# Regrouping the first chunk pair's preparation in an RWKV and Hadamard-MLP kernel: the second chunk's token statistics and normalisation move around the first weight pass, and other steps move with them

## The reference

```python
xn = _layernorm(x)
# attention: token shift, three projections, a running recurrence along the tokens
xr = mu_r * xn + (1 - mu_r) * shifted;  xk = ...;  xv = ...
r, k, v = xr @ Wr.T, xk @ Wk.T, xv @ Wv.T            # 512 x 512 each
wkv = wkv_v4(k, v, wkv_w, wkv_u)                     # max-stabilised scan over the tokens
att = (sigmoid(r) * wkv) @ Wo.T
# MLP: two up projections to 2048, silu gate, Walsh-Hadamard transform, down projection
hidden = fwht(silu(xn @ W1.T) * (xn @ W3.T))
ffn = hidden @ W2.T
out = x + att + ffn
```

## Time and profile before

| | |
|---|---|
| time, median of 3 runs | 2727.08 us (2725.96 to 2729.17) |
| the profiled execution's own time | 2726.61 us |
| its span in the profile | 2724.8 us |
| PE busy | 2665.6 us, 98% |
| DVE busy | 2205.9 us, 81% |
| ACT busy | 1318.0 us, 48% |
| POOL busy | 243.0 us, 9% |
| first product of the first pair starts | 129.99 us into the span |

### The profile page before, as it was taken

One profiled execution on the slowest core, in us unless ns is written; L12 is line 12 of the kernel. 1 busy time (PEld: TensorE's weight loads), 2 busy tenths in 40 slices (PEclk: granted clock), 3 DMA queues, 4 the chain that ended last, 5 costly groups with the idle time before them and its releaser, 6 DMA issues.

```text
span 2724.8 us, 33882 instructions
## 1 busy us (share of the span) xinstructions
PE 2665.6 (98%) x11616; PEld 2181.7 (80%) x11616; DVE 2205.9 (81%) x2962; ACT 1318.0 (48%) x2115; POOL 243.0 (9%) x180
## 2 busy tenths in 40 slices
PE   7998999999999999999999999999999999999999
PEld 5676778888888888888888888888888888888887
DVE  6798987888878888688886888878888788878775
ACT  6655556444544445444464444644455444554442
POOL 3297820000000000000000000000000000000000
PEclk9999999999999999999999999999999999999999
DMA  6787687787878778687787877878687787876777
GB/s 237 279 309 246 239 284 251 251 263 232 273 240 274 241 244 283 226 276 241 250 280 230 269 235 263 271 238 272 220 276 251 250 264 228 272 244 222 226 233 266
DMA packets 244951, 691.50 MB, mean 254 GB/s; under 512 B 31920, under 2 KB 31920, under 8 KB 244272
## 3 DMA queue, kind: packets, MB, share of 16 engines
q1 hardware_dynamic: 244784, 689.34, 76.2%
HBM read 575.94 MB, written 113.30 MB: 253 GB/s over the span
## 4 chain that ended last, share of the span: by engine, by line
PE 87%; DVE 8%; ACT 2%; issue 2%; DMA 1%; POOL 1%; SPq 0%; ACTq 0%; DVEq 0%
PE gamma L863 12%; PE gamma L865 12%; PE gamma L866 12%; PE acc L873 10%; PE acc L875 10%; PE acc L874 10%; PE gamma L945 4%; PE gamma L947 4%; PE gamma L946 4%; PE alpha L866 2%; PE alpha L865 2%; PE alpha L863 2%; PE alpha L946 1%; PE alpha L947 1%; PE alpha L945 1%
## 5 line engine op out<-in xcount | busy, mean ns | idle before, releaser
L1059 ACT ACTIVATE step<-gamma 128x512 f32<-128x512 f32 x512 | 305.7, 597 | 840.9 <-PE gamma L866 817.9
L863 PE MATMUL gamma<-xs_high,wring 128*128 128x512 f32 x1280 | 500.2, 391 | 14.2 <-DVE step L1514 8.3
L865 PE MATMUL gamma<-xs_high,wring 128*128 128x512 f32 x1280 | 498.9, 390 | 0.0
L866 PE MATMUL gamma<-xs_low,wring 128*128 128x512 f32 x1280 | 498.8, 390 | 0.0
L873 PE MATMUL acc<-vring,hid 128*128 128x512 f32 x1232 | 481.5, 391 | 14.2 <-POOL vring L744 6.7
L875 PE MATMUL acc<-vring,hid 128*128 128x512 f32 x1232 | 479.9, 390 | 0.0
L874 PE MATMUL acc<-vring,hid 128*128 128x512 f32 x1232 | 479.9, 390 | 0.0
L863 PEld LDWEIGHTS gamma<-xs_high,wring 128*128 128x128 f32 x1280 | 240.9, 188 | 69.3 <-issue 11.2
L873 PEld LDWEIGHTS acc<-vring,hid 128*128 128x128 f32 x1232 | 231.3, 188 | 68.9 <-issue 14.8
L866 PEld LDWEIGHTS gamma<-xs_low,wring 128*128 128x128 f32 x1280 | 240.8, 188 | 50.2
L865 PEld LDWEIGHTS gamma<-xs_high,wring 128*128 128x128 f32 x1280 | 240.9, 188 | 49.8
(11 more groups left out here) (171 smaller groups left out, 4779.8 us busy)
## 6 DMA issues: line engine op xcount, KB each, us to landing
wring<-u_split SPq DMA_DIRECT2D x336, 512.0 KB, 4.2
vring<-d_split SPq DMA_DIRECT2D x288, 512.0 KB, 4.3
wring<-r_split SPq DMA_DIRECT2D x168, 512.0 KB, 4.2
raw<-spilled SPq DMA_DIRECT2D x160, 256.0 KB, 4.2
spilled<-step SPq DMA_DIRECT2D x128, 256.0 KB, 4.3
wlast<-u_split SPq DMA_DIRECT2D x112, 256.0 KB, 3.3
u_split<-wring SPq DMA_DIRECT2D x48, 512.0 KB, 3.3
res<-x SPq DMA_DIRECT2D x16, 1024.0 KB, 8.0
```

The costliest lines, as they stand in the source:

```text
L863: pe.matmul(bank[:, :], w[:, 0, col], high, start=fresh and kt == 0, stop=False, skip_group_check=True)
L865: pe.matmul(bank[:, :], w[:, 1, col], high, start=False, stop=False, skip_group_check=True)
L866: last = pe.matmul(bank[:, :], w[:, 0, col], low, start=False, stop=kt == 1, skip_group_check=True)
L1059: act.activation(to, bank[:, :], ACT.Copy).then_inc(u_copied, 1)
```

## The change

No operation is added or taken away: all five engines issue the same work, and SP's list is the same row for row. What moves, all of it in the prologue:

1. The second chunk's statistics (`first_stats(1)`) are issued on DVE after step 1, not ahead of step 0. Its diagonals on ACT come after steps 3 and 4, behind the emptying of the first group, not after step 1. Its spreading matmuls come after pass one, not after unit 4, and wait for pass one's banks to be copied. Its `centre` and `scale` move behind stages 3 and 4 of the recurrence, and `mix_first(0, 12)` with them. Pass one waits for two normalised column pairs (`xt_ready`), no longer four.
2. POOL makes the low parts of weight tiles 4 to 8 ahead of its second reciprocal root, not behind it. ACT's high parts go out in another order (tile 2 behind the first high part of the mix, one tile a step, tiles 9 to 11 at steps 6 to 8).
3. Stages 5 and 6 of the recurrence's first quarter move behind steps 10 and 11. The rectification stands after tile 2 of pass one (3 before) and tile 1 of pass two (3 before), the exponentials after tiles 6 and 5 (9 before).
4. `right_made` is issued one piece a step behind steps 17 to 20 (two pieces at 16, one at 17 and at 18 before), `right_lo` at steps 21 to 23. `right_hi` keeps its places. Each product of up step 0 waits only for the right operand that it reads.

```diff
-FIRST_MADE_AT = {16: (0, 1), 17: (2,), 18: (3,)}
+FIRST_MADE_AT = {17: (0,), 18: (1,), 19: (2,), 20: (3,)}
 FIRST_HIGH_AT = {15: (0,), 16: (1,), 17: (2, 3), 18: (4,), 19: (5,), 20: (6,)}
-FIRST_LOW_AT = {18: (0,), 19: (1,), 20: (2,), 21: (3,), 22: (4, 5), 23: (6,)}
+FIRST_LOW_AT = {21: (0, 1), 22: (2, 3), 23: (4, 5, 6)}
...
             inverse_root(0, 0)
             for n in range(12):
                 lo(("r", n))
-                if n == 3:
+                if n == 8:
                     inverse_root(0, 1)
...
+                if j == 0:
+                    wait(pe, xs_hi, s, RIGHT_ORDER.index(RIGHT[piece]) + 1)
+                    wait(pe, xs_lo, s, RIGHT_ORDER.index(RIGHT[piece]) + 1)
                 if piece == 1:
                     if j == 0:
-                        wait(pe, xs_hi, s, 7)
-                        wait(pe, xs_lo, s, 7)
...
             def spread_tokens(h):
                 for a in range(2):
+                    if h:
+                        pe.wait_ge(w2_copied, FT - 1 + a)
...
             def turn_within_tiles():
-                wait(pe, xt_ready, 0, 4)
+                wait(pe, xt_ready, 0, 2)
...
                 r_unit(0, n)
-                if n == SPREAD_AFTER:
-                    spread_tokens(1)
                 if n == PASS_ONE_AFTER:
                     turn_within_tiles()
+                    spread_tokens(1)
...
             mix_first(0, 1)
+            mix_second(0, 0)
             split_high(("r", 2))
-            mix_second(0, 0)
...
                 down_step(-1, n)
                 if n < 3:
-                    split_high(("r", 6 + 2 * n))
-                    split_high(("r", 7 + 2 * n))
-                if n == 1:
-                    diagonals_b(0)
-                    diagonals_b(1)
+                    split_high(("r", 6 + n))
+                if n in (3, 4):
+                    diagonals_b(n - 3)
+                if 6 <= n < 9:
+                    split_high(("r", 3 + n))
...
-                        if j == 3:
+                        if j == 2:
                             rectified(0, 0)
-                        if j == 9:
+                        if j == 6:
                             exponentials(0, 0)
+                    mix_first(0, 12)
...
-                if not with_d and n in (PASS_ONE_AFTER + 1, PASS_TWO_AFTER + 1):
+                if not with_d and n == PASS_ONE_AFTER + 1:
+                    wkv(r, 0, 3)
+                    wkv(r, 0, 4)
+                    centre(r, 1, 0)
+                    scale(r, 1, 0)
+                    mix_item(r, 12)
+                    centre(r, 1, 1)
+                    scale(r, 1, 1)
+                if not with_d and n == PASS_TWO_AFTER + 1:
                     for stage in range(3, 7):
-                        wkv(r, int(n > PASS_TWO_AFTER), stage)
+                        wkv(r, 1, stage)
...
+                    if not with_d and n == PASS_ONE_AFTER + 2:
+                        wkv(r, 0, 5)
+                    if not with_d and n == PASS_ONE_AFTER + 3:
+                        wkv(r, 0, 6)
...
             mix_item(0, 3)
-            first_stats(1)
             for n in range(R_UNITS):
                 down_step(-1, n)
+                if n == 1:
+                    first_stats(1)
```

More of the change, by code:

```diff
@@ L118 @@
 LOW_AT = {9: (0,), 11: (1,), 13: (2,), 16: (3,), 19: (4,), 20: (5,), 21: (6,)}
-SPREAD_AFTER, PASS_ONE_AFTER, PASS_TWO_AFTER = 4, 8, 14
+PASS_ONE_AFTER, PASS_TWO_AFTER = 8, 14
 TURN_ORDER = [W2_LOADS - 1] + list(range(W2_LOADS - 1))
@@ L953, in turn_across_tiles @@
             def turn_across_tiles():
+                wait(pe, xt_ready, 0, 4)
                 for n, j in enumerate(TILES_TURNED):
@@ L1231, in down_step @@
                         mix_second(r, n + MIX_AHEAD)
-                    if n + MIX_AHEAD + 1 < R_UNITS:
+                    if n + MIX_AHEAD + 1 < R_UNITS and (with_d or n != PASS_ONE_AFTER):
                         mix_first(r, n + MIX_AHEAD + 1)
@@ L1288, in _ @@
                         act.activation(fly[1][:, i, :], acc[i % TT][:, :], ACT.Copy).then_inc(w2_copied, 1)
-                        if k == 3:
+                        if k == 1:
                             rectified(0, 1)
-                        if k == 9:
+                        if k == 5:
                             exponentials(0, 1)
-                if n + 3 >= R_UNITS:
-                    split_high(("u", 0, n + 3 - R_UNITS))
+                if 0 <= n + 4 - R_UNITS < 3:
+                    split_high(("u", 0, n + 4 - R_UNITS))
             def pair(s):
@@ L1631, in down_step @@
                         add_residual(s, 0, ADD_A_AT[n])
-                if with_r:
-                    late = not with_d or is_first(s)
-                    centre_at, scale_at = (FIRST_CENTRE_AT, FIRST_SCALE_AT) if late else (CENTRE_AT, SCALE_AT)
+                if with_r and with_d:
+                    centre_at, scale_at = (FIRST_CENTRE_AT, FIRST_SCALE_AT) if is_first(s) else (CENTRE_AT, SCALE_AT)
                     if n in centre_at:
```

## The result

The changed kernel takes 2732.18 us, median of 20 runs (2729.72 to 2737.39), and the kernel before 2727.95 us in the same job (20 runs, 2724.28 to 2731.16). The ratio is 1.0016, 95% interval [1.001, 1.0023]: 4.2 us slower, where 1.9 us faster was forecast. It is within the 0.2% called "no difference" ahead of the run, but outside the range and on the other side. The profiled execution took 2731.28 us, its span is 2729.5 us, 4.7 us longer than before.

A forecast was written before the change was run, and what follows sets the result against it. PE was taken to pace the seven later pairs, DVE beside POOL the first; only the prologue could gain. Pass one 8.5 us ahead shrank to a first product 1.9 ahead: 2727.08 became 2725.2 us, range 2720.0 to 2728.6.

The forecast's parts named there:

- DVE's list between the passes: DVE's work from 61.4 us to the exponents of the second quarter at 84.8: 23.4 us, 2.5 ahead of before.
- The chain behind pass two: Serial ACT and DVE links behind unit 18: unit 20 starts at T + 18.8 after a 5.1 us wait, not 2.10.
- T: Start of unit 15, behind pass two: forecast at 96.7 us against 97.66 before, 1.0 ahead.
- Exponents of pass one: Ready on DVE at 49.5 us, between 47.5 free of POOL and 50.0 with both low parts held.
- The clock in the gap of pass one: PE's gap at tile 7, forecast at 2.3 us; no slow clock behind it in the sum.
- over 18 us: Sign on pass one's length: longer than this means the forecast is wrong on the slow side.
- The first product: First product of pair 0: forecast at T + 31.4 = 128.1 us, 1.9 ahead of 129.99.
- The later pieces find theirs with at most 0.5 of wait: In up step 0, products after the first wait at most 0.5 us for their right operands.
- DVE ends its seven low parts near T + 36: Right operands' low parts end 2 us later against the products, in a stretch where DVE was idle before.
- some 2 us: Allowance for contention of DVE and POOL in the first pair, which can add or take this much.
- Slower: PE's clock: Rival: two gaps inside the passes cost 1.7 us each, 1.5 slower, 2728.6 (0.10); lasting slow clock, 2741 (0.04).
- Nothing arrives: Rival: DVE paces the first pair from its first step, the 1.9 us is given back, 2727.1; chance 0.16.

The follow-up runs named there:

- e3: Changed kernel with the rectifications behind tiles 6 and 4 of the passes and the exponentials behind tiles 10 and 8: 2727.1 us against 2726.41 for the kernel before.
- e1: Changed kernel with sums and low parts of the right operands back at their old steps: 2721.89 us against 2726.41 for the kernel before.
- e2: Changed kernel with PE repeating tile matmuls in the gaps inside both passes: 2730.48 us against 2726.41 for the kernel before.
- e7: Changed kernel with the edits of e1 and e3 together: 2719.59 us against 2726.34 for the kernel before.
- e11: The e7 kernel with the last three `right_hi` one step later (steps 19 to 21): 2720.77 us against 2727.21 for the kernel before.
- e12: Changed kernel with `right_hi` one step later, each one step after the sum it needs (steps 18 to 21): 2731.28 us against 2727.21 for the kernel before.
- e13: Changed kernel with the edits of e9 and e12 together, sums still late: 2726.8 us against 2726.19 for the kernel before.
- e8: The e7 kernel with ACT's high parts of weight tiles 9 to 11 at steps 3 to 5, not 6 to 8: 2720.71 us against 2726.34 for the kernel before.
- e9: Changed kernel with only the low parts of the right operands back at their old steps, sums still late: 2730.52 us against 2726.34 for the kernel before.
- e10: Changed kernel with 20 unused matmuls on PE in the wait ahead of unit 20: 2732.98 us against 2727.21 for the kernel before.

## Why the prediction was wrong, point by point

**What held.** Unit 0 came at 16.52 (16.6 forecast), unit 4 without its wait, unit 5 at 33.06 behind 1.05 us (32.8, 1 us), pass one at 44.23 (44.0). DVE's list between the passes took 64.14 to 87.36, 23.2 us (23.4). The chain behind pass two came as worked out: unit 20 at T + 19.2 with a wait of 5.01 (T + 18.8, 5.1), T being unit 15's start. So the link-by-link walk of ACT and DVE was sound in these three stretches.

**What failed first: T, 3.3 us late (99.98 for 96.7).** The steps:
- Exponents of pass one at 50.73, not the 49.5 taken, and 0.7 outside the bounds of 47.5 to 50.0. The low parts of mixes 10 and 11 took 3.44 us for two, beside POOL, where the earlier trace rows have 0.68 for one alone. 1.2 us.
- The clock in the gap of pass one. The gap was 2.99 us (2.3 forecast), the clock share behind it 0.58. From the exponents to unit 9 it took 13.95 us, not 12.5; where the clock stayed up it took 12.67. 1.3 us.
- Unit 9's 2.7 us lateness moved the spreading of the second chunk and with it DVE's list one for one. Pass two lost another 0.7: from the exponents to unit 15 it took 12.62 us, not 11.9, and 11.33 where the clock stayed up. So the clock cost 1.3 us there too, and the forecast was 0.6 too long without it.

The clock's 2.6 us are most of T's 3.3. The forecast had its price in the earlier trace rows and put it in a rival only ("if each costs what the 2.10 us gap did"), with nothing in the sum. One of its own signs says the same: pass one took from 44.23 to 63.05, 18.8 us, where "over 18 us" was to mean wrong on the slow side. e3 prices the placement as a whole (7.2 us at unit 15).

**What failed second: behind unit 20.** The first product came at 132.97, 13.77 behind unit 20 and not 12.6: 1.2 us, for the slow clock lasted until about 125 us. With T's 3.3 and 0.4 in the chain that makes 4.9 us, from 1.9 ahead to 3.0 behind.

**What failed third, and weighs most in the runs:** "The later pieces find theirs with at most 0.5 of wait", and "DVE ends its seven low parts near T + 36 ... but it had an idle stretch there". The low parts ended at T + 40.6, since beside POOL's 512-column operations each takes 2.3 us and not 1.2 (13.0 for the seven, from 127.61). They cost 1.08 us in up step 0, and POOL's chain 2.69 at up step 1. The prediction allowed "some 2 us" for DVE and POOL in the first pair, outside its sum. Of the 6.65 us of lateness at up step 1, 4.7 are left at 172 us: the kernel before waited 1.36 us for a copy of ACT at 157.90, and the changed one, later already, didn't. The walk followed `right_made` to ACT's copies and stopped. It never asked what stands behind the *fourth* high part on ACT: the split of the first up weights, and behind that POOL's 17 us to up step 1. One engine's stand was costed for one reader and there were two. With both tables put back, e1 is 8.7 us faster, and its first product comes 5.3 us ahead of the kernel before.

**The rivals.** "Slower: PE's clock" named a real mechanism, at 1.7 us a gap where it cost 1.3, but with the clock held up (e2) no gain in the time can be told. "Nothing arrives" came closest: DVE and POOL are what the first pair waits for from its first step, as it said. Its price stopped at zero; being late against the products wasn't only the loss of a lead. The sign would have been right with the sums where they were: e1 is 4.5 us faster than before, though with 5.3 us of lead at the first product and not 1.9.

**What the loss consists of,** as far as the runs show: 8.7 us by the two tables (e1 against the changed kernel), some 3 by the placement of rectification and exponentials (3.5 by e3 against the changed kernel, 2.3 by e7 against e1, each uncertain by about as much), and a gain of 6.8 us by the rest, parts 1 to 3 with the per-product waits (e7). The rest was not taken apart: no run has part 1 or part 2 alone. The 8.7 don't look like a sum of parts: freeing ACT alone 0, spreading the low parts alone 0, both 3.6, and the sums early as well 8.7, each within 2.5 us or so.

**What stays open.** Why POOL took turns with DVE in the changed kernel, e1 and e7 and was shut out in e11, e12 and e13. The order of starting doesn't tell: POOL began 0.03 us ahead of a low part of DVE in e11 and 0.04 ahead of the same one in e7. Why e2 lost its 2.9 us between the first product and `vring`, and e12 5.4 us between up step 1 and `vring`. And why the same gap of PE, 2.99 us in the changed kernel and 2.96 in e1, was followed by a clock share of 0.58 in one and 1.00 in the other.

## What to carry to other kernels

When work is moved later on one engine, follow *every* instruction behind the one that will wait for it, to the last one whose reader matters, not only to the first: here the fourth wait of ACT held no copy, and POOL's first up weight stood behind it. Where one hold is taken away and nothing is gained, don't drop it yet: look for a second hold beside it and take both away in one run, and then check at the marks that the gain came where you think; here it was only in part so. And a lead won early in a prologue counts only if each engine that paces the next stretch keeps it too; filling PE's gaps kept its clock up, and no gain in the time could be told. Last, look at the same mark in several executions of the same code before you price a microsecond by it: here unit 15 alone moved by 2.3 us.

## What the runs showed of the hardware

- **POOL can lose many times in a row.** An operation that takes 1.29 us alone (`vring`, e13 at 132.24) lasted 9.06 us beside seven operations of DVE of 1.15 us each that ran back to back (e12), 7.92 beside the last six of such a run (e13), and 6.92 beside five (e11). Each time it ended 1.1 us behind the last of them. DVE wasn't slowed. In the changed kernel the same two lists took turns, 1.68 us for POOL's first and up to 2.3 for each of DVE's. The Trainium skill (SBUF — State Buffer, Who interferes with whom) has the second to issue wait until the first finishes; that gives one DVE operation and POOL's own, some 2.5 us. The rows of the changed kernel go with it, the 9.06 doesn't.
- **The clock after a gap isn't settled by its length.** Pass one's gap of PE was 2.99 us in the changed kernel, 2.96 in e1 and 2.94 in e13; the granted clock from 53 to 56 us was 0.58, 1.00 and 1.00. Pass two's was 2.13 in the changed kernel and 2.12 in e12, with 0.50 and 1.00 from 91 to 94 us; unit 20's 2.14 in e7 and 2.10 in e8, with 1.00 and 0.75. A slow stretch cost 1.3 us in either pass, and 2.65 where it lasted past 58 us (e9). In this row of e1's windows the share stays at full:

```profile
53.00:56.00 3.00, 2.36 (x6) 1.20 (x7) 0.00 (x0) 3.00 (x7) 0.00 (x0) 1.00 0.53 200
```

- **Matmuls put in a gap held the clock in the long one.** With 20 matmuls ahead of unit 20 the share was 1.00 from 119 to 131 us (e10), where the changed kernel, which waited 5.01 us there, had 0.50 from 119 to 125 and e9 the same. With three repeated tiles in pass one and three in pass two it was 1.00 in the windows behind both gaps (e2); but it was 1.00 behind one of the two without any in e1, e9, e10, e12 and e13, so e2 alone doesn't show it.
